# Decay attention on one Trainium2 core: layer norm on turned rows inside the projection loop, compact blocks of 64 tokens, and one pair of banks for the early products

## The reference

```python
xn = ((x - mean) / sqrt(var + 1e-5))          # the layer norm of the main stream
xn = (xn - mean) / sqrt(var + 1e-5) * ln_g + ln_b   # and the one inside the sublayer
w = sigmoid(xn @ Wx @ Ww + bw);  k = xn @ Wk;  v = xn @ Wv;  r = sigmoid(xn @ Wr)
# per head of 64 channels (2 heads), over time:
state = (1 - w_t)[:, None] * state + k_t[:, None] * v_t[None, :]
out_t = r_t @ state
x = x + out @ Wo
```

## Time and profile before

| | |
|---|---|
| median of 3 executions | 3266.42 us (3254.58 to 3269.03) |
| the profiled execution | 3265.66 us |
| its span in the trace | 3263.9 us |
| first matmul of `layernorm` | 2768.66 us |
| first matmul of the tiles | 2793.95 us |
| first level-2 eviction on DVE | 2847.49 us |
| last merge on DVE begins | 2922.15 us |
| PE turns `kB` | 2928.32 us |

### The profile page before, as it was taken

The page is one execution under the profiler, slowest core; times in us unless marked ns, Lnnn a source line. Parts: engine busy times, 40 slices in busy tenths (PEclk is TensorE's granted clock), DMA queues, the critical chain, the costliest instruction groups (busy, mean ns, idle before and its releaser), DMA issues. The chain is left out here.

```text
span 3263.9 us, 86845 instructions
## 1 busy us (share of the span) xinstructions
PE 3048.2 (93%) x29020; PEld 2370.3 (73%) x29020; DVE 2505.7 (77%) x5782; ACT 2268.4 (70%) x6848; POOL 1947.9 (60%) x3091
## 2 busy tenths in 40 slices
PE   5569999999999999999999999999998999848998
PEld 3448888888888888888888888888774444545444
DVE  5669999999999999999999999999654443664443
ACT  4768888888888888888888888888543333323333
POOL 1588888888888888888888888888710000000000
PEclk8779999999999999999999999999998999959999
DMA  4456776767777767777677767767432322002323
GB/s 100 122 146 169 190 187 170 178 170 179 182 185 178 173 177 178 174 184 182 176 176 175 179 172 187 183 168 177 122 95 84 137 106 103 5 4 76 146 98 123
DMA packets 587924, 482.94 MB, mean 148 GB/s; under 512 B 464492, under 2 KB 504076, under 8 KB 581340
## 3 DMA queue, kind: packets, MB, share of 16 engines
q1 hardware_dynamic: 587484, 477.39, 55.1%
HBM read 285.39 MB, written 191.86 MB: 146 GB/s over the span
## 5 line engine op out<-in xcount | busy, mean ns | idle before, releaser
L1058 DVE SCALAR_TENSOR_TENSOR conv_k<-PP,tk,conv_k 128x256 f32<-128x256 f32 x1536 | 722.6, 479 | 61.0 <-ACT conv_k L893 33.5
L831 POOL TENSOR_TENSOR X<-X,tmp 96x31 f32<-96x31 f32 (+15 forms) x992 | 534.5, 539 | 77.8
L1058 DVE SCALAR_TENSOR_TENSOR conv_v<-PP,tv,conv_v 128x256 f32<-128x256 f32 x1152 | 539.0, 477 | 45.0 <-ACT conv_v L893 35.4
L828 POOL TENSOR_TENSOR tmp<-At,X 96x31 f32<-96x31 f32 (+15 forms) x992 | 486.3, 490 | 63.2 <-DMA At<-n_d 5.0
L1227 PE MATMUL PP<-xn,wk 128*128 128x268 f32 x1024 | 342.2, 418 | 35.9 <-DVE conv_k L1058 27.9
L814 POOL TENSOR_TENSOR rk<-ss,half 96x8 f32<-96x8 f32 x128 | 209.1, 1633 | 175.1 <-DVE ss L1026 175.1
L796 POOL TENSOR_TENSOR Sg<-S,gend 128x512 f32<-128x512 f32 x256 | 266.0, 1039 | 62.0 <-DVE S L1017 62.0
L865 ACT ACTIVATE recA<-TG,es 96x128 f32<-96x128 f32 x1024 | 285.1, 369 | 5.3 <-DVE es L1051 5.3
L893 ACT ACTIVATE conv_k<-PP,tk 128x256 f32<-128x256 f32 x512 | 245.4, 481 | 54.9 <-PE PP L1227 47.6
L1191 PE MATMUL RB<-rhs,Yf 96*96 96x128 f32 x2048 | 269.0, 274 | 14.6 <-DVE rhs L1006 14.5
L857 ACT ACTIVATE recA<-TG 128x128 f32<-128x128 f32 x1024 | 265.5, 272 | 24.6 <-PE TG L1278 24.6
(11 more groups left out here) (280 smaller groups left out, 6751.2 us busy)
## 6 DMA issues: line engine op xcount, KB each, us to landing
kqg_d<-kqgA SPq DMA_DIRECT2D x128, 512.0 KB, 6.3
kqgB<-kqg_d SPq DMA_DIRECT2D x128, 512.0 KB, 4.4
rec_d<-recA SPq DMA_DIRECT2D x128, 480.0 KB, 3.4
recB<-rec_d SPq DMA_DIRECT2D x128, 480.0 KB, 5.8
f1gates<-f1gates_d SPq DMA_DIRECT2D x24, 1024.0 KB, 6.8
f2gates<-f2gates_d SPq DMA_DIRECT2D x24, 1024.0 KB, 6.8
gdec<-gdec_d SPq DMA_DIRECT2D x128, 128.0 KB, 5.6
apk_d<-apkA SPq DMA_DIRECT2D x128, 128.0 KB, 3.3
```

Source lines behind the costliest of these rows:

```text
L828: nc.gpsimd.tensor_tensor(t, At[q % 2][:, j, j + 1:].unsqueeze(2).broadcast_to(sh), X[q % 2][:, j, 0:cols].unsqueeze(1).broadcast_to(sh), ...
L831: nc.gpsimd.tensor_tensor(x, x, t, ALU.subtract).then_inc(sub_ev, 1)
L1058: return nc.vector.scalar_tensor_tensor(acc, src[:, :, j:j + SPAN], w[:, j:j + 1], acc, ALU.mult, ALU.add)
```

## The change

Three things change in the decay sublayer.

1. `layernorm` is gone, with its block and barrier. Tiles of 512 tokens of `xT` are turned by PE into rows with tokens on partitions (`rows_of`, bank 4), DVE sums, centres and later scales the rows (`centre`, `var_eps`, `norm`), ACT squares them with an accumulated sum (`square`), GpSimd (POOL) takes the power of -0.5, PE turns the rows back (`hat`, bank 5), and ACT applies gain and bias (`keep_xn`). All of that stands inside the tile loop, one or two tiles ahead.
2. Compact blocks are 64 tokens (`W`), so level 6 becomes a `near` level: 32 matmuls of 64x64 a step instead of 64 of 32x32, and a DVE eviction of 1024 elements instead of 512.
3. Steps 0 to 7 all use pair 3, since pair 2 holds the turned rows.

```diff
...
-    MASKED = 6
+    MASKED, W = 7, 64
...
-        masks = sb("masks", [128, MASKED, 32])
+        masks = sb("masks", [128, MASKED, W])
-        Pc = sb("Pc", [128, NG, 2, 32])
+        Pc = sb("Pc", [128, NG, 2, W])
...
-        layernorm(nc, g, "ln2", lambda i: g.xT[:, i // 2, TILE * (i % 2):TILE * (i % 2 + 1)],
-                  affine=(gain[:, 0:1], gain[:, 1:2]), fetch=fetch, fetched=(gain_in, 32))
-
+        rows, sq = sb("rows", [128, 2, 4, 128]), sb("sq", [128, 4, 128])
+        nm, var, rs = (sb(n, [128, 2, 4]) for n in ("nm", "var", "rs"))
+        mhalf = sb("mhalf", [128, 4])
...
-        pair_of = lambda n: 2 + n % 2 if n < 2 * B else n % 4
+        pair_of = lambda n: 3 if n < 2 * B else n % 4
+        turned, hatted = (bank[i].rearrange("p (a d) -> p a d", a=4) for i in (4, 5))
+        x_of = lambda i: g.xT[:, i // 2, TILE * (i % 2):TILE * (i % 2 + 1)]
+        xn_of = lambda i: g.xn[:, i // 2, PAD + TILE * (i % 2):PAD + TILE * (i % 2 + 1)]
...
         @block.tensor
         def _(pe):
+            def rows_of(i):
+                if i >= NT:
+                    return
+                need(pe, cent_ev, i - 1)
+                for a in range(4):
+                    last = nc.tensor.transpose(turned[:, a, :], x_of(i)[:, a * 128:(a + 1) * 128], g.ident[:, :])
+                last.then_inc(rows_mm, 1)
+
+            def hat(i):
+                if i >= NT:
+                    return
+                pe.wait_ge(hat_ev, i + 1)
+                need(pe, xn_ev, i - 1)
+                for a in range(4):
+                    last = nc.tensor.transpose(hatted[:, a, :], rows[:, i % 2, a, :], g.ident[:, :])
+                last.then_inc(hat_mm, 1)
+
             def tile(i):
-                x = g.xn[:, i // 2, PAD + TILE * (i % 2):PAD + TILE * (i % 2 + 1)]
+                x = xn_of(i)
+                rows_of(i + 2)
+                pe.wait_ge(xn_ev, i + 1)
                 need(pe, f_ev, i - 1)
                 mm(bank[0], w[:, 0, :], x, start=True, stop=True).then_inc(zx, 1)
                 need(pe, k_ev, i - 1)
                 mm(bank[1], w[:, 2, :], x, start=True, stop=True).then_inc(k_mm, 1)
                 need(pe, r_ev, i - 1)
                 mm(bank[2], w[:, 4, :], x, start=True, stop=True).then_inc(r_mm, 1)
+                hat(i + 1)
                 pe.wait_ge(zx_ev, i + 1)
                 mm(bank[0], w[:, 1, :], z1[:, i % 2, :], start=True, stop=True).then_inc(z_mm, 1)
                 need(pe, v_ev, i - 1)
...
-                    if pair_of(n) < 2:
-                        for ev in (k_ev, r_ev, f_ev, v_ev):
+                    if pair_of(n) < 3:
+                        for ev in (k_ev, r_ev, f_ev, v_ev, xn_ev, cent_ev):
                             pe.wait_ge(ev, NT)
...
-                        for c in range(4):
-                            t0 = (b * NGB + q) * 128 + 32 * c
-                            o = pair[pair_of(n)][32 * c:32 * c + 32, h, 32 * q:32 * q + 32]
-                            last = mm(o, kB[64 * h:64 * h + 64, t0:t0 + 32], rF[64 * h:64 * h + 64, t0:t0 + 32], start=True, stop=True)
+                        for c in range(0, 128, W):
+                            t0 = (b * NGB + q) * 128 + c
+                            o = pair[pair_of(n)][c:c + W, h, W * q:W * q + W]
+                            last = mm(o, kB[64 * h:64 * h + 64, t0:t0 + W], rF[64 * h:64 * h + 64, t0:t0 + W], start=True, stop=True)
                 last.then_inc(p_mm, 1)
...
+            rows_of(0)
+            rows_of(1)
+            hat(0)
             pe.wait_ge(loaded, 16 * len(loads))
...
-            pe.wait_ge(spread_ev, 4 * B)
+            pe.wait_ge(spread_ev, 128 // W * B)
...
         @block.scalar
         def _(act):
+            def square(i):
+                if i >= NT:
+                    return
+                act.wait_ge(cent_ev, i + 1)
+                need(act, sq_ev, i - 1)
+                for a in range(4):
+                    last = nc.scalar.activation(sq[:, a, :], rows[:, i % 2, a, :], ACT.Square, accum_out=var[:, i % 2, a:a + 1])
+                last.then_inc(sq_ev, 1)
+
+            def keep_xn(i):
+                if i >= NT:
+                    return
+                act.wait_ge(hat_mm, i + 1)
+                nc.scalar.activation(xn_of(i), bank[5], ACT.Identity, scale=gain[:, 0:1], bias=gain[:, 1:2]).then_inc(xn_ev, 1)
+
             def tile(i):
                 act.wait_ge(zx, i + 1)
                 need(act, z_mm, i - 2)
                 nc.scalar.activation(z1[:, i % 2, :], bank[0], ACT.Copy).then_inc(zx_ev, 1)
                 act.wait_ge(r_mm, i + 1)
                 nc.scalar.activation(rF[:, TILE * i:TILE * (i + 1)], bank[2], ACT.Sigmoid).then_inc(r_ev, 1)
+                keep_xn(i + 1)
                 act.wait_ge(z_mm, i + 1)
                 nc.scalar.activation(F[:, TILE * i:TILE * (i + 1)], bank[0], ACT.Sigmoid, scale=-1.0, bias=neg_bw[:, :]).then_inc(f_ev, 1)
+                square(i + 2)
...
-                for c in range(4):
-                    o = slice(32 * c, 32 * c + 32)
+                for c in range(0, 128, W):
+                    o = slice(c, c + W)
                     nc.scalar.activation(P[o, G, :, o], Pc[o, G, :, :], ACT.Copy).then_inc(spread_ev, 1)
 
+            square(0)
+            square(1)
+            act.wait_ge(gain_in, 32)
+            keep_xn(0)
             act.wait_ge(nb_ev, 1)
             for i in range(NT):
                 tile(i)
-            act.wait_ge(cleared, 1)
-            for b in range(B):
-                far(MASKED, b)
+            act.wait_ge(cleared, NT)
             for b in range(B):
                 spread(b)
...
-            nc.gpsimd.memset(P[:, :, :, :], 0.0).then_inc(cleared, 1)
+            nc.gpsimd.memset(mhalf[:, :], -0.5).then_inc(mhalf_ev, 1)
+            pool.wait_ge(mhalf_ev, 1)
+            for i in range(NT):
+                pool.wait_ge(ve_ev, i + 1)
+                need(pool, hat_ev, i - 2)
+                nc.gpsimd.tensor_tensor(rs[:, i % 2, :], var[:, i % 2, :], mhalf[:, :], ALU.pow).then_inc(rs_ev, 1)
+                nc.gpsimd.memset(P[:, 4 * i:4 * i + 4, :, :], 0.0).then_inc(cleared, 1)
...
         @block.vector
         def _(dve):
+            EPS = 1e-5
+            spread = lambda t, i: t[:, i % 2, :].unsqueeze(2).broadcast_to([128, 4, 128])
+
+            def centre(i):
+                if i >= NT:
+                    return
+                dve.wait_ge(rows_mm, i + 1)
+                nc.vector.tensor_reduce(nm[:, i % 2, :], turned, AX.X, ALU.add).then_inc(sum_ev, 1)
+                dve.wait_ge(sum_ev, i + 1)
+                nc.vector.tensor_scalar(nm[:, i % 2, :], nm[:, i % 2, :], -1.0 / D, None, ALU.mult).then_inc(mean_ev, 1)
+                dve.wait_ge(mean_ev, i + 1)
+                need(dve, hat_mm, i - 2)
+                nc.vector.tensor_tensor(rows[:, i % 2, :, :], turned, spread(nm, i), ALU.add).then_inc(cent_ev, 1)
+
+            def var_eps(i):
+                if i >= NT:
+                    return
+                dve.wait_ge(sq_ev, i + 1)
+                nc.vector.tensor_scalar(var[:, i % 2, :], var[:, i % 2, :], (1.0 + EPS) / D, EPS * EPS, ALU.mult, ALU.add).then_inc(ve_ev, 1)
+
+            def norm(i):
+                if i >= NT:
+                    return
+                dve.wait_ge(rs_ev, i + 1)
+                nc.vector.tensor_tensor(rows[:, i % 2, :, :], rows[:, i % 2, :, :], spread(rs, i), ALU.mult).then_inc(hat_ev, 1)
+
             def tile(i):
+                var_eps(i + 1)
+                centre(i + 2)
+                norm(i + 1)
                 dve.wait_ge(k_mm, i + 1)
                 nc.vector.tensor_copy(kB[:, TILE * i:TILE * (i + 1)], bank[1]).then_inc(k_ev, 1)
                 dve.wait_ge(v_mm, i + 1)
...
-                src = pair[pair_of(n)][:, :, 0:32 * NGB].rearrange("p h (q t) -> p h q t", t=32)
-                mask = masks[:, l, :].unsqueeze(1).unsqueeze(1).broadcast_to([128, 2, NGB, 32])
+                src = pair[pair_of(n)][:, :, 0:W * NGB].rearrange("p h (q t) -> p h q t", t=W)
+                mask = masks[:, l, :].unsqueeze(1).unsqueeze(1).broadcast_to([128, 2, NGB, W])
...
             nc.vector.memset(S[:, 0, :, :], 0.0).then_inc(z_ev, 1)
+            centre(0)
+            centre(1)
+            var_eps(0)
+            norm(0)
             dve.wait_ge(loaded, 16 * len(loads))
             nc.vector.tensor_scalar(neg_bw[:, :], bw[:, :], -1.0, None, ALU.mult).then_inc(nb_ev, 1)
```

More of the change, by code:

```diff
@@ L57, in constants @@
     a = np.arange(128)
-    s, t = a[:, None] % 32, np.arange(32)[None, :]
+    s, t = a[:, None] % 64, np.arange(64)[None, :]
     bm = [(s == t).astype(np.float32)]
-    for l in range(5):
+    for l in range(6):
         h = 1 << l
@@ L115, in _ @@
             sp.wait_ge(stored, 64)
[L118 to L181, removed]
-                nc.scalar.activation(xc[:, i % 4, :], cen[i % 2][:, :], ACT.Copy).then_inc(copied, 1)
-            def root(i):
-                act.wait_ge(varied, i + 1)
```

(33 more changed lines are left out.)

5 lines of the change are left out of this document (added).

## The result

| | before | after |
|---|---|---|
| time, median of 20 runs | 3265.78 us (3254.58 to 3269.03) | 3255.82 us (3249.64 to 3260.96) |
| ratio, 95% interval | | 0.9974 [0.9967, 0.9981] |
| profiled execution (span) | 3265.66 (3263.9) | 3252.41 (3250.6) |

The forecast was 3260, within 0.5% of before; measured are 10 us less by the medians, 0.3%. The two spans differ by 13.3 us. 3.2 of them lie ahead of the change: the sublayer's first matmul stands at 2768.66 before and at 2765.42 after, behind code that is the same. So from here on the stages are read from that matmul on, each by its own start and end.

A forecast was written before the change was run, and what follows sets the result against it. Bounds before: PE's instruction supply in the products, ACT's copies behind the last merge, PE in the tiles. Products -6.3, tail -5.4, norm and tiles +5.6 sum to -6.1 us: 3260 us, range 3247 to 3278.

The forecast's parts named there:

- Products: Level 2 to last merge: DVE becomes the limit at 3.07 us a step, 75.4 to 69.1 us, gain 6.3.
- Tail: Behind DVE's last merge: ACT's remaining copies no longer delay PE's turn of `kB`, gain 5.4 us.
- Lead-in: Start of the sublayer: transposes, centring, power and first norm take 7.8 us to the first projection.
- Tiles 0 and 1, to `hat(3)`: First tiles: PE-bound at 5.8 us, tile 0's projections charged double (7.8); 16.7 us in all.
- Loops: Four rounds to `hat(7)`: each closes through DVE, 8.4 or 9.1 us against 5.74 before; 34.9 us.
- End: From `hat(7)` to the first level-2 eviction: 21.3 us, some 1.5 of it from the one pair.
- Clock: PE's pauses before `hat(4)` to `hat(7)` and at the end: five, one in three dipping at 2.2 us; 3.7 us.
- signs of being wrong: Profile after: DVE idle before evictions, PE clock 0.50 through the tiles, or a first level-2 eviction before 2847.
- the first: Rival in norm and tiles: no clock dip, first tile not slow, 3252 us; chance beyond the bound 0.12.
- The second: Rival in the products: the issue wait hangs on the step and stays, +15.1 us, 3281; chance 0.04.
- The third: Rival in the tiles: pauses hold PE at 1.2 GHz in all eight, 3289 us; chance 0.08.
- the fourth rival: Products: 64x64 matmuls over 48 ns a record make PE the limit; 3276 us at 60 ns; chance 0.04.

The follow-up runs named there:

- e1: The kernel before with compact blocks of 64 tokens alone, keeping its own norm and two pairs of banks: 3254.2 us, ratio to before 0.9974.
- e3: The changed kernel with each 64x64 product of a near step issued as two of 64x32: 3276.1 us, ratio to before 1.0033.
- e4: The kernel before with ACT's spread of each sequence put ahead of its level-6 copies: 3260.2 us, ratio to before 0.9988.
- e8: e6 with a bank of its own for the second tile's turned rows in the lead-in: 3247.3 us, ratio to before 0.996.
- e6: The changed kernel with DVE taking the next tile's five norm instructions ahead of the eviction and merge before them: 3248.8 us, ratio to before 0.9965.
- e5: e1 with the early products on one pair of banks: 3253.4 us, ratio to before 0.9971.
- e2: The changed kernel with blocks of 32 tokens again and level 6 by ACT: 3266.3 us, ratio to before 0.9999.
- e7: The changed kernel with each merge's third instruction (F) on POOL from level 2 on, PE waiting only for the first two: 3243.8 us, ratio to before 0.9947.
- e9: The changed kernel with each merge's third instruction, still on DVE, multiplying only the last column of each odd block of F: 3247.0 us, ratio to before 0.996.

## Why the prediction was right or wrong

The sum was -6.1, the stages gave -9.2. By its own terms:

- **Products, gain 6.3; measured 4.6.** The mechanism is shown (e1, e3). The eviction was mis-sized: it starts the next instruction after 1.22 us, not 1.14, which is 20 x 0.08 = 1.6 of the 1.7 us missed. The extrapolation took the second 512 elements from a plain multiply; the row it needed was a `COPY_PREDICATED` of 1024. PE's bound was good: 1.97 to 1.99 us a step against 2.0 to 2.4.
- **Tail, gain 5.4; measured 5.3.** Shown by e4.
- **Lead-in, 7.8; measured 9.5** (2765.42 to 2774.89). Missed was a wait that the change adds: `rows_of(1)` needs the one bank that `centre(0)` still reads, 1.71 us. e8 took it away and got 1.2 back.
- **Tiles 0 and 1, to `hat(3)`, 16.7; measured 16.4. Loops, 34.9; measured 34.15.** Both as worked out, step by step; e6 shows that the loops were a round trip through DVE.
- **End, 21.3; measured 19.6.** 0.9 of the 1.7 us is the first part: near(1, 2)'s eviction started 9.2 us behind `hat(7)` and not 10.1, and the prediction's own prices add up to about 9.1 there. The two parts behind it were 0.4 and 0.5 too long. The 1.5 us charged to the shared pair are not there (e5): while PE waits for the bank, DVE is at the merge that PE needs next anyway.
- **Clock, 3.7; measured 0 in the loops.** The step that failed. The four pauses ahead of `hat` came out at 1.5 and 2.4 us, close to the forecast, and the clock stayed at 1.00. The fifth, 3.10 us, was followed by the low clock, but what came late by it was one near step and not `hat`, `z` and `v`: near(1, 3)'s eviction started 1.63 us behind its first matmul, where near(1, 2)'s took 1.23 at full clock. That is 0.4 us, and it is within the 19.6 above. In e3 a pause of 2.45 us ahead of `hat(7)` did lower the clock, at 1.6 us instead of the 2.2 charged, so such pauses can cost this, but they are no rule: in e2, e7 and e9 none of the four did, with pauses up to 2.48 us. The frequency, one in three, was a guess; it came out at one of 20 in these five kernels. What decides it wasn't found.

+1.7 for the lead-in, -0.3, -0.75, -1.7 and -3.7 make -4.8 (79.6 against 84.4); products and tail give 1.8 back; that is the -3.1 between forecast and stages. So the mechanisms of products, tail and loops held, and the size was two thirds of what came; that it was no further off owes something to luck, since the lead-in and the products missed one way and the end and the clock the other. Of the signs of being wrong, one came in by its letter: the first level-2 eviction stood at 2844.98, earlier than 2847. By its own start it didn't: 3.2 us are the earlier first matmul, and 79.6 us behind the first matmul of before would be 2848.2.

Of the rivals, the first was half right: no dip in the loops, but tile 0 was slow, its first two projection groups at half the clock (2.07 and 1.91 us) and the third in part (1.43). The second fell with the steps of 3.14 us, and again in e3. The rule of the Trainium skill (page Runtime: NRT & Kernel Launch, section Instruction fetch mechanics), that crossing a block is "mostly hidden", holds for the tiles of before, where a step and a tile take 5.7 us and PE shows no such wait; it doesn't hold in the products, where PE waited for "issue" 1.7 to 2.3 us at nearly every block of before and 1.1 to 1.8 in e3 at full clock. The third and the fourth rival fell with the clock at 1.00 in the tiles and 31 ns a record in the products. Two numbers behind the fourth were off, and nothing hangs on them: 122 records in 4.8 us are 39 ns and not 37, and 70 ns a record would give 3288 and not 3286.

## What to carry to other kernels

Where PE waits for "issue" at even distances, count instructions, not columns: fewer and larger matmuls help, and a faster PE does nothing: in e3 bursts of 2.1 and of 3.7 us came equally far apart. When a change adds work to an in-order engine, its place in that engine's order decides what it costs: with the same five instructions behind eviction and merge the norm inside the projections gained nothing, and ahead of them 7 us. And price each part by its own start and end in the trace, for a total can agree by accident, as with the pair of banks.
